# One GpSimd instruction instead of four for the division of a gated chunk by its block scales

## The reference

```python
x = x + attention(layernorm(x))        # 16 heads of 64, softmax over 2048 keys, output projection and bias
x = x + ffn(layernorm(x))              # 128 -> 352 (gate and up) -> 128 (down)

def fp4_quant_dequant(x):              # blocks of 16 along the last axis
    xb = x.reshape(shape[:-1] + (shape[-1] // 16, 16))
    scale = maximum(max(abs(xb), axis=-1, keepdims=True) / 6.0, 1e-12)
    xn = xb / scale
    idx = searchsorted([0.25, 0.75, 1.25, 1.75, 2.5, 3.5, 5.0], abs(xn))
    return (GRID[idx] * sign(xn) * scale).reshape(shape)

def ffn(x):                            # every operand of every product is quantised
    h = silu(q(x) @ q(w_gate).T) * (q(x) @ q(w_up).T)
    return q(h) @ q(w_down).T
```

## Time and profile before

| | us |
|---|---|
| median of 3 runs | 1322.88 (1321.32 to 1325.54) |
| the profiled execution | 1325.37 |
| its span in the trace | 1323.5 |
| busy: PE, DVE, ACT, POOL | 1260.0, 886.0, 881.9, 1060.1 |
| mean granted TensorE clock | 0.981 of full speed |

### The profile page before, as it was taken

The page is one execution under the profiler, slowest core; times in us unless marked ns, Lnnn a source line. Parts: engine busy times, 40 slices in busy tenths (PEclk is TensorE's granted clock), DMA queues, the critical chain, the costliest instruction groups (busy, mean ns, idle before and its releaser), DMA issues.

```text
span 1323.5 us, 24786 instructions
## 1 busy us (share of the span) xinstructions
PE 1260.0 (95%) x7417; PEld 661.2 (50%) x7417; DVE 886.0 (67%) x2378; ACT 881.9 (67%) x1246; POOL 1060.1 (80%) x528
## 2 busy tenths in 40 slices
PE   4999999999999999999999999999999998988767
PEld 3555555555455555555455555555455554443336
DVE  6666666677666667677566667677666667666598
ACT  5767676777667666677667676777666776664444
POOL 4488888988888888988788888988888889777547
PEclk9999999999999999999999999999999999998888
DMA  2000000000000000000000000000000000000001
GB/s 64 2 10 1 1 2 10 1 1 2 4 10 1 1 2 10 1 1 2 4 10 1 1 2 10 1 1 2 1 4 1 2 1 1 1 1 1 1 1 32
DMA packets 45953, 6.68 MB, mean 5 GB/s; under 512 B 37344, under 2 KB 45664, under 8 KB 45808
## 3 DMA queue, kind: packets, MB, share of 16 engines
q1 hardware_dynamic: 45584, 4.41, 2.6%
q0 software_dynamic: 224, 0.54, 0.1%
HBM read 3.75 MB, written 1.05 MB: 4 GB/s over the span
## 4 chain that ended last, share of the span: by engine, by line
PE 82%; POOL 7%; issue 5%; DVE 4%; ACT 1%; DMA 0%; POOLq 0%; SPq 0%; DVEq 0%; ACTq 0%
PE o_ps L1315 32%; PE s_ps L1156 24%; PE mx_ps L1178 8%; PE mx_ps L1171 4%; PE misc_ps L1293 3%; PE misc_ps L1305 2%; POOL acc_pool L588 2%; PE misc_ps L1143 2%; POOL acc_pool L587 2%; PE misc_ps L1121 2%; PE s_ps L1164 1%; POOL scaled L542 1%; PE misc_ps L1122 1%; PE misc_ps L1123 1%; POOL hq L572 1%
## 5 line engine op out<-in xcount | busy, mean ns | idle before, releaser
L591 POOL TENSOR_TENSOR acc_pool<-acc_pool,probs 128x1024 f32<-128x1024 f32 x308 | 742.2, 2410 | 47.5 <-POOL acc_pool L591 40.5
L708 ACT ACTIVATE probs<-s_ps 128x1024 f32<-128x1024 f32 x512 | 524.9, 1026 | 79.3 <-PE s_ps L1156 38.0
L891 DVE CUSTOM_DVE_ANT_0 summed<-mx_ps,rise 128x512 bf16<-128x512 f32 x503 | 344.8, 685 | 290.2 <-issue 246.2
L1315 PE MATMUL o_ps<-probs,vv 128*64 128x512 f32 x2048 | 499.1, 607 | 8.9 <-ACT probs L708 8.8
L629 ACT ACTIVATE rise<-mx_ps 128x512 f32<-128x512 f32 x503 | 299.9, 596 | 258.4 <-PE mx_ps L1171 253.3
L1315 PEld LDWEIGHTS o_ps<-probs,vv 128*64 128x64 f32 x2048 | 127.1, 137 | 232.7 <-issue 179.9
L1178 PE MATMUL mx_ps<-k_hi,q_hi 64*128 64x512 f32 x503 | 224.3, 446 | 6.4 <-issue 3.8
L1171 PE MATMUL mx_ps<-k_raw,q_hi 64*128 64x512 f32 x503 | 224.7, 447 | 4.8 <-ACT rise L629 3.6
L1156 PE MATMUL s_ps<-q_hi,k_hi 64*128 64x512 f32 x1024 | 206.3, 396 | 3.1 <-ACT probs L708 3.1
L1156 PE MATMUL s_ps<-q_hi,k_lo 64*128 64x512 f32 x1024 | 204.6, 393 | 0.0
L1156 PE MATMUL s_ps<-q_lo,k_hi 64*128 64x512 f32 x1024 | 204.3, 392 | 0.0
(11 more groups left out here) (181 smaller groups left out, 1169.4 us busy)
## 6 DMA issues: line engine op xcount, KB each, us to landing
mrow<-neg_max SPq DMA_DIRECT2D x256, 0.5 KB, 2.0
wqkv<-in_L_attn_w_qkv SPq DMA_DIRECT2D x8, 192.0 KB, 2.9
y<-in_L_attn_x SPq DMA_DIRECT2D x4, 256.0 KB, 4.5
out<-y SPq DMA_DIRECT2D x4, 256.0 KB, 2.5
wo<-in_L_attn_w_out SPq DMA_DIRECT2D x8, 64.0 KB, 1.9
wx<-in_L_ffn_w_down POOLq DMA_DIRECT2D x1, 176.0 KB, 5.8
wx<-in_L_ffn_w_gate POOLq DMA_DIRECT2D x1, 128.0 KB, 4.7
wx<-in_L_ffn_w_up POOLq DMA_DIRECT2D x1, 128.0 KB, 5.1
```

What stands on the lines that cost most here:

```text
L591: pool.tensor_tensor(acc, first, probs[:, j % P_BUFS, :, :], ALU.add) \
L708: act.activation(probs[:, j % P_BUFS, :, :], s_ps[:, j % 2, :, :], ACT.Exp, scale=SCALE) \
L891: dve.tensor_tensor_reduce(summed[:, s % 2, :], mx_bank(h, pair), rise[:, h, :], 1.0, LOWEST, ALU.add, ALU.max, part_max[:, slot:slot + 1] ...
L1315: ins = pe.matmul(o_ps[DH * h:DH * (h + 1), :], vv[par(w)][:, j, DH * h:DH * (h + 1)], probs[:, j % P_BUFS, h, :], start=(j == 0), stop=(j ...
```

## The change

`over_scale` no longer cuts a chunk of gated products in quarters. It issues one instruction over all 1408 values for h0, h1 and h2, and two over 704 each for h3. It signals `f_div` at the same places in the data as before. `times_scale` is left as it is, and so are the single instructions for the groups of x and the weights.

```diff
-                for i in range(pieces(n)):
-                    cols = slice(i * width // pieces(n), (i + 1) * width // pieces(n))
-                    some = slice(i * nb // pieces(n), (i + 1) * nb // pieces(n))
-                    ins = pool.tensor_tensor(by_block(scaled[buf(n)][:, cols]), by_block(src[:, cols]),
-                                             each_block(binv[:, n % 3, some], nb // pieces(n)), ALU.mult)
-                    if i == pieces(n) - 1 or (n == len(QUANTS) - 1 and i == pieces(n) // PARTS - 1):
-                        ins.then_inc(f_div, 1)
+                parts = PARTS if n == len(QUANTS) - 1 else 1
+                for i in range(parts):
+                    cols = slice(i * width // parts, (i + 1) * width // parts)
+                    some = slice(i * nb // parts, (i + 1) * nb // parts)
+                    pool.tensor_tensor(by_block(scaled[buf(n)][:, cols]), by_block(src[:, cols]),
+                                       each_block(binv[:, n % 3, some], nb // parts), ALU.mult).then_inc(f_div, 1)
```

## The result

| | before | changed |
|---|---|---|
| median of 21 runs, us | 1323.72 | 1326.09 |
| profiled span, us | 1323.5 | 1324.5 |
| POOL's instructions for one division, h0 to h2 | 4 of 0.78 to 2.16 us | 1 of 2.59 us |

The changed kernel takes 1.0018 of the time before (95% interval 1.0011 to 1.0026), which is 1.5 to 3.4 us more. In a later comparison the ratio was 1.0015 (1.0004 to 1.0026). The forecast was +1.6 us, a difference that the prediction held too small to tell from no change, with the line drawn at 0.3%.

What follows compares the result with a forecast made beforehand. DVE was taken to bound the tail, taking turns with POOL, one instruction at a time. The terms -0.9 + 1.36 + 0.98 + 0.1 gave +1.6 us, so 1324.4 us on the median 1322.88; range 1321.8 to 1327.0.

Steps and rivals of the forecast that it cites:

- The length: POOL's division of h0, h1 and h2: one instruction of 1408 values takes 2.60 us.
- the rival at the accumulation's rate: All four divisions: the long instruction takes 3.22 us for 2.60, +4.1 us in total, 1326.9 us; chance 0.09.
- The hold: DVE's first rounding step beside POOL's long division is held to its end: +1.81 us at h0, +1.82 at h1.
- The first rival: A long POOL instruction holds DVE no longer than a quarter does: -3.3 us in total, 1319.6 us; chance 0.07.
- h0: Division beside x3's rounding: DVE is held longer, but its idle time before tile 7's product goes; -0.9 us.
- h1's division: Beside h0's rounding: DVE's first step is held +1.82 us, later steps give some back; +1.36 us.
- h2's: Division beside h1's rounding: the same hold, partly given back at DVE's wait for tile 15's silu; +0.98 us.
- h3: Division in halves beside h2's rounding: two longer turns, then shorter steps once POOL has no divisions; +0.1 us.
- h0 gives nothing back: At h0, tile 7's silu is bound by TensorE or an earlier product: +2.4 us in total, 1325.3 us; chance 0.10.
- The delays vanish: In the tail, DVE's added holding is given back at waits: no change, 1322.9 us; chance 0.08.
- Which of the two begins first decides little: At h1: had DVE begun first, POOL would hold a later DVE step instead, by as much.

Runs made afterwards that it cites:

- the run with DVE first: Changed kernel, with POOL's divisions of h1 and h2 waiting until DVE's first rounding step goes first; tail 50.98 us, ratio 1.0011 to the kernel before.
- h0 whole: Kernel before, with only the division of h0 as one instruction and the others in quarters; tail 48.76 us, ratio 0.9991.
- silu first: Kernel before, quarters kept, with tile 7's silu ahead of h0's absolute values in ACT's list; tail 48.04 us, ratio 0.9995.
- the halves: Kernel before, with every chunk of gated products divided in two instructions of 704 values; tail 50.52 us, ratio 1.0006.

## Why the prediction was right

- The length: 2.60 forecast, 2.59 measured, and the rival at the accumulation's rate (3.22) is out. The line through the 352 and 1120 rows held; the estimate from the Trainium skill (GPSIMD Engine Reference, "Elementwise — side-by-side cycle accounting"), some 3.1 us, did not.
- The hold: L821 took 2.65 and 3.12 us, forecast 2.66 and 3.14. The first rival (a long instruction does not hold DVE longer) fell with that, and the run with DVE first shows the same hold from the other side.
- h0: -0.9 forecast, 9.19 to 8.30 = -0.89. h1's division: +1.36 forecast, 10.39 to 11.74 = +1.35. h2's: +0.98 forecast, 10.79 to 11.73 = +0.94. h3: +0.1 forecast, 19.64 to 19.78 = +0.14. Sum 1.6 forecast, 1.54 measured. (The forecast's terms as they are printed add up to 1.54; with 0.89 for h0 and 0.12 for h3, as they were worked out, to 1.57.)
- The rival "h0 gives nothing back" is out: the silu was ready, at 1273.85. "The delays vanish" is out: the end moved by what DVE lost.
- What I did not see: h2's +0.98 stands on a wait of 0.46 us that goes with TensorE's lower clock. In kernels that have the full clock there (h0 whole, silu first) that wait is not to be had, and a whole division costs 1.3 at h2 too: with the silu first, 10.41 to 11.74. That this term came out right rests on the wait being there in both profiles of the kernel before. In the changed kernel the clock is 1.00 at that place, so its own profile does not say whether the wait went because DVE was later, as forecast, or by the clock; the halves, with 0.66 and no wait, show that being later is enough. "Which of the two begins first decides little" was right in kind, at 0.28 us a chunk and not "by as much".
- In the time itself the change came out at the upper side, 2.4 us for 1.6; the interval reaches down to 1.5. The median of 1326.09 lies 1.7 above the forecast of 1324.4, and 0.8 of that is the kernel before, whose median rose from 1322.88 to 1323.72 with more runs.

## What to carry to other kernels

When an instruction's duration varies with no semaphore in sight, lay the two engines' timelines side by side and look for ends at a fixed distance from each other: then it is the other's length that counts, not its own busy time. Joining instructions to save their fixed part pays nothing if the engine that sets the end can slip in between them. With one form for all chunks quarters were the best length here (50.01, for 51.55 whole, 50.52 in halves, 51.25 in eighths), since too short pieces get one turn for each step of the other and fall behind. But the best form differs from place to place: with h0 alone whole the tail is 48.76, as DVE had idle time to give up there. And a wait that a change removes may be removable for nothing by the order of a list.

## What was not expected of the hardware

- How long an instruction is held is exact enough to plan by: it ended 0.75 us (1408 values in the tensor_scalar), 1.48 (two float32 operands) or 2.44 (POOL, 1408) behind the other's end, in all the kernels whose rows stand above.
- TensorE's granted clock falls at the same place of the tail in repeated runs of one kernel (0.66 in the same 5 us, twice), and not at that place in a kernel whose division of h0 is another: 1.00 with h0 whole.
- One execution of the kernel before took 1330.82 us, 8 above its median. Its tail was 50.04, like the other's. Its clock was 0.83 in the first 60 us for 0.97 in the first profile of that kernel; DVE's first reciprocal behind it began 7.6 us later (67.77 for 60.15), and the tail 5.4 us later. The window of that execution:

```profile
0.00:60.00 60.00, 41.13 (x176) 28.50 (x178) 34.78 (x136) 33.09 (x58) 17.97 (x26) 0.83 0.13 36
```

  The profiled execution of the changed kernel with the silu first, 1331.78 us, has 0.83 there too. Why the clock was lower in these two stays open.
